# Summing two experts' rows in the transfer or on VectorE, at the end of an adaLN block with experts

## What is computed

```python
h = _layernorm(x) * (1 + cb) + sb
logits = xf @ Wg                                   # 8 experts
top_vals, top_idx = jax.lax.top_k(logits, 2)       # two experts for each token
top_w = jax.nn.softmax(top_vals, axis=-1)
h = relu(einsum('td,edf->tef', xf, W1) + b1)       # 128 -> 512
sparse = einsum('te,tef,efd->td', combine, h, W2) + combine @ b2
shared = relu(xf @ Ws1 + bs1) @ Ws2 + bs2          # the shared expert, all tokens
x = x + gb * (sparse + shared)
```

## Time and profile before

| | |
|---|---|
| median of 3 runs | 668.44 us (668.13 to 669.33) |
| time of the profiled run | 667.99 us |
| its span, first to last instruction | 666.3 us |
| PE busy | 617.9 us (93%) |
| DVE busy | 456.4 us (68%) |
| ACT busy | 403.0 us (60%) |
| POOL busy | 345.8 us (52%) |
| mean granted TensorE clock | 0.978 of full speed |

### The profile page before, as it was taken

One profiled execution on the slowest core, in us unless ns is written; L12 is line 12 of the kernel. 1 busy time (PEld: TensorE's weight loads), 2 busy tenths in 40 slices (PEclk: granted clock), 3 DMA queues, 4 the chain that ended last, 5 costly groups with the idle time before them and its releaser, 6 DMA issues.

```text
span 666.3 us, 12536 instructions
## 1 busy us (share of the span) xinstructions
PE 617.9 (93%) x4306; PEld 559.7 (84%) x4306; DVE 456.4 (68%) x1438; ACT 403.0 (60%) x645; POOL 345.8 (52%) x342
## 2 busy tenths in 40 slices
PE   4998899999999998979949989999999999999996
PEld 3787888898989887868738879999999999999995
DVE  6769797989898969764653447667655445453498
ACT  3787678787878757624414646557556566473551
POOL 3541616757575647757370156566666565566100
PEclk9999999999999999889978999999999999999999
DMA  8340000110101011101044746665665566510593
GB/s 261 124 157 2 1 2 21 33 37 29 40 29 41 29 37 33 44 29 45 25 155 123 239 133 179 214 189 174 192 217 186 186 201 206 184 63 31 217 409 139
DMA packets 32158, 77.67 MB, mean 117 GB/s; under 512 B 7198, under 2 KB 13630, under 8 KB 31968
## 3 DMA queue, kind: packets, MB, share of 16 engines
q1 hardware_dynamic: 22736, 59.48, 27.3%
q0 software_dynamic: 8640, 16.93, 7.4%
q10 hardware_dynamic: 720, 0.47, 0.2%
HBM read 54.52 MB, written 23.25 MB: 117 GB/s over the span
## 4 chain that ended last, share of the span: by engine, by line
PE 61%; DVE 20%; issue 7%; ACT 5%; another core or an unknown queue 4%; DMA 1%; POOL 1%; POOLq 0%; SPq 0%; DVEq 0%; ACTq 0%
PE value L2006 15%; PE value L1828 10%; PE score L1800 8%; PE score L1801 8%; PE score L1802 8%; PE misc L2006 5%; DVE work L1198 3%; PE misc L1841 2%; PE value L2066 2%; DVE rows_all L1221 2%; DVE rows_all L1208 2%; DVE stats L1096 1%; ACT work L898 1%; ACT work L852 1%
## 5 line engine op out<-in xcount | busy, mean ns | idle before, releaser
L786 POOL DMA_INDIRECT rows_z<-tile_y,tags x142 | 149.3, 1052 | 123.1 <-DVE tile_y L1613 37.1
L1800 PE MATMUL score<-h_hi,h_lo 128*128 128x512 f32 (+1 forms) x252 | 96.5, 383 | 4.5 <-issue 4.3
L1828 PE MATMUL value<-w_ring,work 128*128 128x129 f32 x768 | 94.7, 279 | 3.0 <-issue 2.2
L1828 PEld LDWEIGHTS value<-w_ring,work 128*128 128x128 f32 x768 | 91.3, 194 | 6.5 <-issue 3.7
L1802 PE MATMUL score<-h_hi,h_lo 128*128 128x512 f32 (+1 forms) x252 | 91.5, 363 | 0.0
L850 ACT ACTIVATE work<-work 128x1024 f32<-128x1024 f32 x64 | 67.2, 1050 | 34.0 <-DVE work L1198 31.5
L898 ACT ACTIVATE work<-score,w_ring 128x512 f32<-128x512 f32 (+1 forms) x96 | 53.0, 614 | 53.5 <-PE score L1802 41.7
L636 POOL DMA_INDIRECT rows_x<-work,slot x64 | 63.2, 987 | 42.4 <-issue 16.3
L1801 PE MATMUL score<-h_hi,h_lo 128*128 128x512 f32 (+1 forms) x228 | 81.8, 359 | 0.4 <-issue 0.2
L1198 DVE TENSOR_TENSOR work<-score,lw 128x1024 f32<-128x1024 f32 x64 | 76.5, 1215 | 7.1 <-PE score L1802 4.3
L898 ACT ACTIVATE work<-score,w_shared 128x512 f32<-128x512 f32 x64 | 40.0, 684 | 53.2 <-PE score L1802 26.7
(11 more groups left out here) (272 smaller groups left out, 1253.3 us busy)
## 6 DMA issues: line engine op xcount, KB each, us to landing
w_ring<-packs SPq DMA_DIRECT2D x24, 578.0 KB
rows_all<-packs SPq DMA_DIRECT2D x23, 578.0 KB
lw<-rows_x SPq DMA_DIRECT2D x24, 260.0 KB
res<-x SPq DMA_DIRECT2D x7, 512.0 KB, 7.5
h_t<-rows_z SPq DMA_DIRECT2D x3, 1024.0 KB, 11.0
mod<-mod_rows SPq DMA_DIRECT2D x1, 2560.0 KB, 8.6
rows_z<-tile_y,tags POOLq DMA_INDIRECT x142
rows_all<-rows_z SPq DMA_DIRECT2D x2, 1024.0 KB, 13.0
```

The source lines that it names most:

```text
L786: nc.gpsimd.indirect_dma_start(rows_z[:, :], bass.IndirectOffsetOnAxis(ap=tags[j % SLOTS][:, k, 0:1].bitcast(I32), axis=0), tile_y[j % RIN ...
L1800: nc.tensor.matmul(out, a_lo, b_hi, start=True, stop=False)
L1828: ins = nc.tensor.matmul(value[:, s // 3, c0:c0 + D + 1], prob[:, t % 4, s * P:(s + 1) * P], normal[b % 3][:, t, :], start=(t == 0 and s % ...
```

## The change

Seven of the eight batches no longer get both rows by one load. SP loads only the first expert's rows (`load_first`, which increments the new `z_first[b]`). GpSimd waits for that and then issues a transfer of the second expert's rows onto the same place with `accum_op` add (`add_second`), which increments `z_loaded[b]`. Of batch 4 this holds for the second half only; its first half and batch 0 are loaded as before and summed on VectorE. On VectorE the sum of z0 and z1 is left out in `add_shared`, `last_rows_into_result` and in `add_front` of all but batch 0. `last_rows_into_result` has a wait for `z_loaded` of its own. In VectorE's list `add_front(2)`, `add_front(3)` and `last_rows_into_result(7)` each stand one shared tile sooner, and `fin_parts` (the order of the stores) follows.

```diff
--- before.py
+++ after.py
@@ -382,6 +382,7 @@
         z_half_loaded = sem("z_half_loaded")
         y_sent = [sem(f"y_sent{i}") for i in range(RING)]
         z_loaded = [sem(f"z_loaded{i}") for i in range(B)]
+        z_first = [sem(f"z_first{i}") for i in range(B)]
         early_hi = sem("early_hi")
         early_lo = sem("early_lo")
         part_ready = sem("part_ready")
@@ -402,8 +403,9 @@
                 rows_all[:, 0:2 * S], rows_all[:, 2 * S:4 * S], w_ring[:, 0:2 * S]]
         z_order = [b for i in range(B // 2) for b in (B // 2 + i, i)]
         z_slot = {b: z_at[i % len(z_at)] for i, b in enumerate(z_order)}
-        fin_parts = [p for i in range(B // 2 - 1) for p in ((B // 2 + i, 0, K), (i, 0, G), (B // 2 + i, K, G))]
-        fin_parts += [(B // 2 - 1, 0, G), (B - 1, 0, K), (B - 1, K, K + 2), (B - 1, K + 2, G)]
+        half = B // 2
+        fin_parts = [p for i in range(2) for p in ((half + i, 0, K), (i, 0, G), (half + i, K, G))]
+        fin_parts += [(2, 0, G), (half + 2, 0, K), (3, 0, G), (half + 2, K, G), (half + 3, 0, K), (half + 3, K, K + 2), (half + 3, K + 2, G)]
 
         block = ctx.enter_context(nc.Block())
 
@@ -509,9 +511,13 @@
             for par in range(RING):
                 sp.wait_ge(y_sent[par], sent_in_all(par))
 
-            def load_results(b, on=None, n0=0, n1=S):
-
-                sp.dma_start(z_slot[b].rearrange("p (k n) -> p k n", k=2)[:, :, n0:n1], z_v[b][:, :, n0:n1]).then_inc(on or z_loaded[b], 16)
+            def load_results(b, on, n0=0, n1=S):
+
+                sp.dma_start(z_slot[b].rearrange("p (k n) -> p k n", k=2)[:, :, n0:n1], z_v[b][:, :, n0:n1]).then_inc(on, 16)
+
+            def load_first(b, n0=0):
+
+                sp.dma_start(z_slot[b][:, n0:S], z_v[b][:, 0, n0:S]).then_inc(z_first[b], 16)
 
             def store(i):
 
@@ -521,15 +527,15 @@
                              res[:, b * G + g0:b * G + g1, :].rearrange("p g d -> p (g d)")).then_inc(stored, 16)
 
             load_results(z_order[0], z_half_loaded, 0, TILE)
-            load_results(z_order[1])
-            load_results(z_order[0], None, TILE, S)
+            load_results(z_order[1], z_loaded[z_order[1]])
+            load_first(z_order[0], TILE)
             for b in z_order[2:len(z_at)]:
-                load_results(b)
+                load_first(b)
             for i in range(len(fin_parts)):
                 store(i)
                 if i == 2:
                     for b in z_order[len(z_at):]:
-                        load_results(b)
+                        load_first(b)
             sp.wait_ge(stored, 16 * len(fin_parts))
 
 
@@ -808,6 +814,15 @@
                     pool.wait_ge(y_ready, ROW_TILES)
                 send_rows(ROW_TILES - 1, k)
 
+            def add_second(b, n0=0):
+
+                pool.wait_ge(z_first[b], 16)
+                nc.gpsimd.dma_start(z_slot[b][:, n0:S], z_v[b][:, 1, n0:S], accum_op=ALU.add).then_inc(z_loaded[b], 16)
+
+            add_second(z_order[0], TILE)
+            for b in z_order[2:]:
+                add_second(b)
+
 
         @block.scalar
         def _(act):
@@ -1700,12 +1715,11 @@
                 b, half = divmod(FRONT + i, 2)
                 dve.wait_ge(z_loaded[b], 16)
                 dve.wait_ge(down_ready, FRONT + ROW_TILES + i + 1)
-                z0, z1 = (z_slot[b][:, k * S + half * TILE:k * S + half * TILE + TILE].rearrange("p (g d) -> p g d", d=D) for k in range(2))
+                z0 = z_slot[b][:, half * TILE:half * TILE + TILE].rearrange("p (g d) -> p g d", d=D)
                 gate = mod[:, b:b + 1, 4, :].to_broadcast([P, K, D])
                 r = res[:, b * G + K * half:b * G + K * half + K, :]
                 nc.vector.tensor_tensor(z0, yacc[(i + 2) % RING].rearrange("p (k d) -> p k d", k=K), z0, ALU.add).then_inc(y_evac, 1)
                 dve.wait_ge(y_evac, FRONT + ROW_TILES + i + 1)
-                fin(nc.vector.tensor_tensor(z0, z0, z1, ALU.add))
                 fin(nc.vector.tensor_tensor(z0, z0, gate, ALU.mult))
                 nc.vector.tensor_tensor(r, r, z0, ALU.add).then_inc(fin_ready, 1)
 
@@ -1716,7 +1730,8 @@
                 z0, z1 = (z_slot[b][:, k * S:(k + 1) * S].rearrange("p (g d) -> p g d", d=D) for k in range(2))
                 gate = mod[:, b:b + 1, 4, :].to_broadcast([P, G, D])
                 r = res[:, b * G:b * G + G, :]
-                fin(nc.vector.tensor_tensor(z0, z0, z1, ALU.add))
+                if b == z_order[1]:
+                    fin(nc.vector.tensor_tensor(z0, z0, z1, ALU.add))
                 fin(nc.vector.tensor_tensor(z0, z0, gate, ALU.mult))
                 nc.vector.tensor_tensor(r, r, z0, ALU.add).then_inc(fin_ready, 1)
 
@@ -1732,9 +1747,9 @@
             def last_rows_into_result(i):
 
                 b, half = divmod(FRONT + i, 2)
-                z0, z1 = (z_slot[b][:, k * S + half * TILE:k * S + half * TILE + TILE].rearrange("p (g d) -> p g d", d=D) for k in range(2))
+                z0 = z_slot[b][:, half * TILE:half * TILE + TILE].rearrange("p (g d) -> p g d", d=D)
                 r = res[:, b * G + K * half:b * G + K * half + K, :]
-                fin(nc.vector.tensor_tensor(z0, z0, z1, ALU.add))
+                dve.wait_ge(z_loaded[b], 16)
                 fin(nc.vector.tensor_tensor(z0, z0, mod[:, b:b + 1, 4, :].to_broadcast([P, K, D]), ALU.mult))
                 fin(nc.vector.tensor_tensor(r, r, z0, ALU.add))
 
@@ -1758,12 +1773,12 @@
             add_shared(2)
             add_front(1)
             add_shared(3)
+            add_front(2)
             add_shared(4)
-            add_front(2)
+            add_front(3)
             add_shared(5)
-            add_front(3)
+            last_rows_into_result(7)
             add_shared(6)
-            last_rows_into_result(7)
             last_shared_part(7, 0, yacc[(7 + 2) % RING])
             last_shared_part(7, 1, xt_ps)
```

## The result

The changed kernel is slower: 675.89 us against 668.29 us (medians of 6 runs each), ratio 1.0115, 95% interval 1.0096 to 1.0134. The forecast was 666.1 with a range up to 672.4, so it failed in its sign and in its range. The first rival had said 675.0 for an accumulated byte at twice the price of a plain one; the range stopped at a ratio of 1.7 and so left that end out.

A forecast was written before the change was run, and what follows sets the result against it. VectorE's tail was taken to bound the kernel, beside TensorE's floor and the DMA engines. Tile 3 at 652.2 plus 9.64 ends VectorE at 661.8, 2.3 us sooner: 667.99 becomes 665.7, plus 0.45 gives 666.1; range 665.2 to 672.4.

The forecast's parts named there:

- first rival: Slower: in the tail, accumulation reads twice and fills the DMA engines; 670.6 us at ratio 1.5, 675.0 at 2; chance 0.30.
- unknown price: DMA cost of an accumulated byte against a plain one: ratio 1 taken, 2 from above; each tenth delays tile 3 by 0.89 us.
- the prediction's sum: Tile 3's landing from 8.5 MB at 2.73 us a MB gives 652.2; 9.64 us of VectorE work behind it gives 661.8.
- stores that no longer stand behind it: Three stores, 1 MB, share the engines with tile 3's accumulation, moving its landing from 649.5 to 652.2.
- The delay of batch 4: First accumulated tile whole at 632.3 to 633.6, wanted by add_shared(1) at 632.7: under 1 us late, absorbed later.
- The floor: TensorE's end 660.28 plus 0.04 and 0.84 for the last half part: VectorE ends no sooner than 661.2; at most 2.9 us won.
- the work removed: Sums z0 + z1 leave six add_shared, last_rows and three add_front on VectorE: 8.9 us.
- the pace of GpSimd's issues: Seven added transfers of 128 rows, priced by an indirect transfer's 0.98 us, once 1.41: 7 to 10 us in all, no cost.
- the 9.64 us behind tile 3: VectorE's work after tile 3 lands: add_front(3) 2.40, add_shared(5) 2.05, last rows 1.46, add_shared(6) 2.05, parts 1.68.
- What the order costs: add_front(3) one shared tile sooner needs tile 3 before add_shared(5), add_shared(6) and last_rows; a shared tile is 2.05 us.
- Rival 4: The 5.26 us VectorE stand before 616.9 changes: data sooner, but TensorE's floor holds, nothing under 665.2; no chance of its own.

## Why the prediction was wrong

- **The failed step is the unknown price.** The prediction took an accumulated byte at ratio 1. It argued from the earlier trace rows that reading SBUF and writing it side by side cost nothing. That comparison could not show it: it had no transfer that accumulates, only plain loads and plain stores beside each other. (The stretch read as loads alone also held a store, issued at 628.45; from 626 to 628.4, where it did not, the rate was 399 GB/s, so the comparison comes out the same.) Measured, 208 against 414 GB/s, ratio 2.0, and 2.1 beside plain loads. By the prediction's sum the step from ratio 1 to 2 is worth 8.9 us at tile 3; taking the addition out gave back 8.5. With ratio 2 the sum gives tile 3 at 661.1, VectorE's end at 670.7 and 675.0 us; the profile has 662.3, 671.94 and 675.81 us, the median 675.89. The Trainium skill, "Collectives: The Full Stack" (why ReduceScatter is half of AllGather), says that an addition emits two read descriptors per chunk and halves the rate. The rate agrees with this trace: 1.93 there, in a collective, 2.0 here. That two reads are the cause is not shown here: GpSimd's queue counts 576 packets for 2.10 MB with the addition as without.
- **The right price stood in the prediction** as its first rival, with chance 0.30, and the page was cited for it. It lost to a comparison of rows that did not contain the operation.
- **A term that was near in size by luck.** For ratio 1 the prediction added 2.7 us at tile 3, for stores that no longer stand behind it. The plain transfers showed 3.7, but the run without the chain of waits took them all away: it is the waits for the first rows, not the stores. So the nearness of 661.1 to 662.3 is in part luck.
- **The delay of batch 4** was put at under 1 us beyond what VectorE wants. VectorE stood 6.15 us for it, and 3.68 with plain transfers on chip 11. The prediction took the time to landing from a scatter of 64 KB on a quiet queue, 2.68 us; at full engines the 256 KB took 7.8 us accumulating and 6.5 plain.
- **The floor** of 661.2 was not put to the test on the first chip, where VectorE ended at 671.94, long after TensorE. On the others VectorE ended 0.9 to 1.0 us behind TensorE in five kernels that had the data in time or nearly (the prediction's count: 0.04 + 0.84), and 2.0 us behind with batch 7 alone accumulated.
- **Right** were the work removed, 8.9 us, the pace of GpSimd's issues (0.84 to 0.98 us) and the 9.64 us behind tile 3: 671.94 - 662.29 = 9.65.
- **What the order costs** was priced by name in the prediction, one shared tile of 2.05 us, and was 1.3 to 2.0 us with late data. What it gains was missed for the chips on which VectorE stands for TensorE.
- **Rival 4** asked what happens if the stand before 616.9 goes. On the other chips it was gone, and the changed kernel's loss was smaller: 1.0057 instead of 1.0115.

## What to carry to other kernels

An accumulating transfer is not a free addition: here it took the DMA engines twice a plain one's time, so look for its place among bytes that move while these engines have gaps and that are needed late. And before work is taken off an engine, see whether a new order of its list gets to the same floor; here it did. When an operation is in no row of the trace, look whether the nearest row has the same number of reads and writes before you take its price. And a share of 100% tells nothing of the rate: put GB/s beside it.

## What was not expected of the hardware

- The engines' share stays at 1.02 to 1.07 whether they move 414 or 208 GB/s; only the rate tells the two apart.
- GpSimd's issue of an accumulating transfer of 128 rows of 4 KB takes 0.84 to 0.98 us in the kernel, a plain one 0.54 to 0.60. Four accumulating ones in a row, with no waits between them, took 3.59 us together, four plain ones 2.22.
- The same kernel took 668 us in the case's own measurement and 634 us on chips 0 and 11, at a granted clock of 0.978 and 0.994. Both profiles of the case have waits that are put down to no engine of the core, in the kernel before the longest 9.4 us, mostly between 250 and 380 us and once, 5.28 us, in the last expert tile. No profile of the experiments has one. What they are was not settled. The balance between TensorE and the transfers differs by some 4 us between the two, and with it the worth of each edit.
